# Cross-attention, feed-forward and experts on one core: GpSimd's sequence in a chunk of the first phase

## The reference

```
q, k, v = layernorm(x) @ Wq.T, ctx @ Wk.T, ctx @ Wv.T        # 16 heads of 16, per token
attn    = softmax(q @ k.T / 4)                               # 16 x 16 within one token
x       = x + (attn @ v, heads outermost, reshaped to [128, 256]) @ Wp.T + bp
n       = layernorm(x)
shared  = (silu(n @ sfc1.T) * (n @ sfc2.T)) @ sfc3.T         # 512 hidden
w, e    = top 2 of n @ gate_w.T over 16 experts, softmax over the two
moe     = sum over the two of w * (silu(n @ w1[e].T) @ w2[e].T)   # 128 hidden
out     = x + moe + shared
```

## Time and profile before

| what | value |
|---|---|
| median of three runs | 1799.47 us (1798.7 to 1801.85) |
| the profiled execution | 1810.45 us, span 1808.6 us |
| TensorE busy | 1503.7 us (83%) |
| VectorE busy | 1330.9 us (74%) |
| GpSimd busy | 1348.2 us (75%) |
| ScalarE busy | 725.1 us (40%) |
| DMA | 344.75 MB, mean 191 GB/s |

### The profile page before, as it was taken

The page is one execution under the profiler, slowest core; times in us unless marked ns, Lnnn a source line. Parts: engine busy times, 40 slices in busy tenths (PEclk is TensorE's granted clock), DMA queues, the critical chain, the costliest instruction groups (busy, mean ns, idle before and its releaser), DMA issues.

```text
span 1808.6 us, 50645 instructions
## 1 busy us (share of the span) xinstructions
PE 1503.7 (83%) x17109; PEld 1317.5 (73%) x17110; DVE 1330.9 (74%) x3306; ACT 725.1 (40%) x1346; POOL 1348.2 (75%) x1253
## 2 busy tenths in 40 slices
PE   5499999999999999999999999976677766677674
PEld 4478888778887878778877888765566766677674
DVE  7578888888888888888888888875355555546553
ACT  3244454444544454445444454432232333233231
POOL 4267777777778777777777787866677877778786
PEclk9699999999999999999999999998788898888887
DMA  8788988888889888888888978855777776677673
GB/s 195 142 194 186 183 168 205 198 172 173 181 209 181 180 166 204 194 175 172 180 218 175 180 158 211 168 134 205 238 225 220 228 231 197 188 214 223 210 231 112
DMA packets 945834, 344.75 MB, mean 191 GB/s; under 512 B 824088, under 2 KB 898730, under 8 KB 940288
## 3 DMA queue, kind: packets, MB, share of 16 engines
q1 hardware_dynamic: 901680, 216.53, 58.4%
q0 software_dynamic: 33600, 92.91, 14.5%
q10 hardware_dynamic: 10512, 34.79, 5.9%
HBM read 200.37 MB, written 148.15 MB: 193 GB/s over the span
## 4 chain that ended last, share of the span: by engine, by line
PE 36%; DVE 18%; issue 16%; SPq 9%; POOL 8%; DMA 8%; ACT 4%; DVEq 1%; POOLq 0%; ACTq 0%
PE bank_a L1172 3%; DVE w_sb L786 3%; ACT xn L631 3%; PE bank_y L1159 3%; PE bank_y L1157 3%; PE bank_y L1158 3%; PE bank_a L1157 3%; DVE th L871 2%; DVE ctx_lo L898 2%; PE bank_a L1159 2%; DVE ln_stats L915 2%; PE bank_a L1158 2%; PE bank_u L1157 2%; SPq L337 2%; PE bank_a L1311 2%
## 5 line engine op out<-in xcount | busy, mean ns | idle before, releaser
L400 POOL DMA_INDIRECT slots<-xn,slot_i x256 | 281.3, 1099 | 100.1 <-issue 55.3
L1111 DVE SCALAR_TENSOR_TENSOR v_area<-bank_y,tail,v_area 128x256 f32<-128x256 f32 x288 | 124.4, 479 | 213.5 <-PE bank_y L1159 107.5
L1400 PE MATMUL bank_a<-ident,k_area 128*128 128x128 f32 x576 | 92.8, 313 | 115.9 <-DMA k_area<-slots 115.4
L521 POOL DMA_INDIRECT sums<-v_area,tail x144 | 144.8, 1005 | 57.2 <-issue 35.6
L521 POOL DMA_INDIRECT out<-v_area,tail x144 | 144.8, 1005 | 51.8 <-issue 33.7
L1400 PEld LDWEIGHTS bank_a<-ident,k_area 128*128 128x128 f32 x576 | 74.2, 160 | 126.6 <-DMA k_area<-slots 126.6
L409 POOL DMA_INDIRECT sums<-v_area,slot_i x128 | 128.0, 1000 | 33.1 <-issue 29.2
L1157 PE MATMUL bank_y<-wsh_out_hi,hid_hi 128*128 128x256 f32 x512 | 143.0, 279 | 1.3 <-POOL hid_lo L431 1.3
L1158 PE MATMUL bank_y<-wsh_out_lo,hid_hi 128*128 128x256 f32 x512 | 142.8, 279 | 0.0
L1159 PE MATMUL bank_y<-wsh_out_hi,hid_lo 128*128 128x256 f32 x512 | 142.7, 279 | 0.0
L1157 PE MATMUL bank_y<-w_hi,xn_hi 128*128 x288 | 104.5, 363 | 41.4 <-POOL xn_lo L513 30.0
(11 more groups left out here) (222 smaller groups left out, 5322.8 us busy)
## 6 DMA issues: line engine op xcount, KB each, us to landing
k_area<-slots SPq DMA_DIRECT2D x288, 129.0 KB
v_area<-sums SPq DMA_DIRECT2D x288, 128.0 KB
kv_dram<-w_sb SPq DMA_DIRECT2D x32, 1024.0 KB
x_sb<-in_x_in SPq DMA_DIRECT2D x32, 512.0 KB
ctx_sb<-in_ctx_t SPq DMA_DIRECT2D x32, 512.0 KB
q_dram<-q_sb SPq DMA_DIRECT2D x32, 512.0 KB
k_area<-kv_dram SPq DMA_DIRECT2D x256, 64.0 KB
w_sb<-q_dram SPq DMA_DIRECT2D x256, 64.0 KB
```

Of the source, the lines that this page charges most:

```text
L400: pool.indirect_dma_start(slots[j], bass.IndirectOffsetOnAxis(ap=slot_i[:, par, j, i:i + 1], axis=0), row_of[j][:, i, :], None).then_inc(S ...
L521: pool.indirect_dma_start(target, bass.IndirectOffsetOnAxis(ap=tail[:, r, t, 1 - j:2 - j].bitcast(u32), axis=0), y_ring[:, r, t, :], None, ...
L1111: st = nc.vector.scalar_tensor_tensor(out=y_ring[:, r, t, :], in0=Y[t // 2][:, t % 2 * C:(t % 2 + 1) * C], scalar=tail[:, r, t, j:j + 1], ...
L1400: last = nc.tensor.transpose(A[t // 2][:, t % 2 * C + k * P:t % 2 * C + (k + 1) * P], x_ring[:, r, t, CHANNEL[j] + k * P:CHANNEL[j] + (k + ...
```

## The change

In GpSimd's body the base scatters are cut into one ahead of `xn2_split` and three behind `x_split`; `x_split` moves from the end of body c - 1 (as `x_split(c + 2)` there) to the front of body c (as `x_split(c + 1)`), behind `xn2_split`; all four base scatters stand ahead of `scale_probs`. Of the eight slot scatters three instead of four stand ahead of the first `hid_split`, and one now stands behind the last. On ScalarE `x_round` moves in the same way, from `turned_out` to between the two exponentials of the next body. The prologue no longer has the subtraction and the rounding of chunk 2. No instruction is added or removed, and all data and buffers stay as they were.

```
--- before.py
+++ after.py
@@ -451,35 +451,36 @@
             ln2_power(0)
             ln1_power(2, False)
             ctx_split(2)
-            x_split(2)
-
-            def body(c, par, first, ahead_2):
+
+            def body(c, par, first, ahead, ahead_2):
+                if not first:
+                    scatter_base(c - 2, par, range(1))
                 xn2_split(c - 1)
-                if not first:
-                    scatter_base(c - 2, par, range(3))
+                if ahead:
+                    x_split(c + 1)
+                if not first:
+                    scatter_base(c - 2, par, range(1, BPC))
                 scale_probs(c)
-                if not first:
-                    scatter_base(c - 2, par, range(3, BPC))
-                scatter(c - 1, 1 - par, SCATTERS[:4])
+                scatter(c - 1, 1 - par, SCATTERS[:3])
                 hid_split(c - 1, range(1))
+                scatter(c - 1, 1 - par, SCATTERS[3:4])
+                hid_split(c - 1, range(1, 2))
                 scatter(c - 1, 1 - par, SCATTERS[4:5])
-                hid_split(c - 1, range(1, 2))
-                scatter(c - 1, 1 - par, SCATTERS[5:6])
                 hid_split(c - 1, range(2, 3))
-                scatter(c - 1, 1 - par, SCATTERS[6:])
+                scatter(c - 1, 1 - par, SCATTERS[5:7])
                 hid_split(c - 1, range(3, SB))
+                scatter(c - 1, 1 - par, SCATTERS[7:])
                 ln2_power(c)
                 if ahead_2:
                     ln1_power(c + 2, False)
                     ctx_split(c + 2)
-                    x_split(c + 2)
-
-            body(1, 1, True, True)
+
+            body(1, 1, True, True, True)
             with pool.Fori(2, CHUNKS - 3, 2) as c:
-                body(c, 0, False, True)
-                body(c + 1, 1, False, True)
-            body(CHUNKS - 2, 0, False, False)
-            body(CHUNKS - 1, 1, False, False)
+                body(c, 0, False, True, True)
+                body(c + 1, 1, False, True, True)
+            body(CHUNKS - 2, 0, False, True, False)
+            body(CHUNKS - 1, 1, False, False, False)
 
             def pads(j):
 
@@ -631,12 +632,10 @@
                     st = nc.scalar.activation(xn2[:, i, XN2], h2[:, par, i, :], ACT.Identity, bias=ln2_shift[:, i:i + 1], scale=ln2_rstd[:, i:i + 1])
                 st.then_inc(S["xn2_ready"], 1)
 
-            def turned_out(c, ahead_2):
+            def turned_out(c):
                 for k in range(KT):
                     act.wait_ge(S["t2_full"], at(KT, c, k + 1))
                     nc.scalar.activation(xn2_t[:, k, :], XN2T_BANKS[k][:, :], ACT.Copy).then_inc(S["t2_out"], 1)
-                if ahead_2:
-                    x_round(c + 2)
                 for k in range(KT):
                     act.wait_ge(S["t2_out"], at(KT, c, k + 1))
                     st = nc.scalar.activation(xn2_hi[:, k, :], xn2_t[:, k, :], ACT.Copy)
@@ -664,10 +663,13 @@
             o_round(0)
             ctx_round(2, 0)
             ln2(0, 0, True)
-            turned_out(0, True)
+            turned_out(0)
 
             def body(c, par, first, ahead, ahead_2):
-                exps(c, range(2))
+                exps(c, range(1))
+                if ahead:
+                    x_round(c + 1)
+                exps(c, range(1, 2))
                 gap_exps(c - 1)
                 if ahead:
                     project_out(c + 1, False)
@@ -682,7 +684,7 @@
                     act.wait_ge(S["hid_split"], at(SB, c - 1, 2))
                     load_x_t(c + 2)
                 ln2(c, par, False)
-                turned_out(c, ahead_2)
+                turned_out(c)
 
             body(1, 1, True, True, True)
             with act.Fori(2, CHUNKS - 3, 2) as c:
```

## The result

The changed kernel takes 1959.46 us (median of 4 runs, 1953.35 to 1962.18) against 1799.09 us: a ratio of 1.0886, 95% interval 1.0863 to 1.0908. It is slower by 160 us, where +8.7 was forecast. The profiled execution took 1953.35 us, with a span of 1951.5. One execution of the version with the late gap, further down, took 3583 us, twice its fellows, and is in no ratio here.

The account below looks back on a forecast made before the run. No engine was full, so the order of waits decides, VectorE's queue and `xn` setting the chunk. (0.43 - 0.14) x 30 = +8.7 us gave a median of 1808.2 us; 8 in 10 from 1784 to 1832.

Parts of the forecast that it names:

- Term A: VectorE's small steps from `gap` to L792: holds mostly handed on, -0.14 us a chunk, bounds -0.7 and +0.96.
- term B: `xn` waits for the landing of the slot scatter behind the last `hid` split: +0.43 us a chunk.
- so I take 2.8: Last slot scatter, beside `x_t`'s load: landing taken as 2.8 us after its end, at 633.14 against 632.71 for `xn`.
- the bound of 4.8 us: Last slot scatter's landing: at most 4.8 us after its end, or `xn` would have waited; +2.4 us a chunk there.
- the four: The rival outcomes for the whole kernel: 1787.5, 1795.3, 1841 and 1816 us, chances 0.28, 0.12, 0.12 and 0.08.
- Rival 4: GpSimd's `xn_lo` and `x_lo` not parted by ScalarE's wait (0.8 us), `gap` held: +17, 1816 us; chance 0.08.
- Rival 1: VectorE's holds really go, at `hot` or L861: -0.65 to -0.7 us a chunk there, 1787.5 us; chance 0.28.

Follow-up runs that it names:

- the late gap: The kernel before, with VectorE's `gap` subtraction moved behind the indices and `hot`, a one-column memset in its old place: 1788.84 us, 0.9904.
- the front alone: The changed kernel with all slot scatters where they were before, the new GpSimd front and ScalarE's rounding of x kept: 1814.87 us, 1.0023.
- the late gap and the base scatters together: The kernel before with `gap` behind `hot` and all base scatters ahead of `scale_probs`; three or four slot scatters ahead of the first `hid` split: 0.9807, 0.9811.

## Why the prediction was wrong

**Right.** Term A step by step: `gap` 0.17; `hot` held to 2.25 us; `hot_sum` in its pause at 0.18; the section up to L792 nearly unmoved. I had -0.14 us for the section, and it is +0.05. The rule of the Trainium skill ("SBUF — State Buffer", "SBUF: two separate sides"), two SBUF inputs against a GpSimd subtraction, agrees with the trace here: 2.25 us. The one detail that fell otherwise: the last hold came at `slot_i` (in some chunks at `slot_back`), a few steps ahead of `gap_1`, and ended where it was to end, with `scale_probs`. The mechanism of term B was right as well: `xn` stands behind the eighth scatter's landing.

**Wrong.** The step that failed is the price in term B, "so I take 2.8": the landing came some 5.6 us after the scatter's end (mean over the chunks), and `xn`'s wait grew by 3.44 us, not 0.43. My rows were of a scatter whose packets were out before the x_t load moved. I saw that the new one would lie beside that load, and took a value at the end of the unhindered ones. Even the bound of 4.8 us was none: it bounds the landing of a scatter in front of the load, not of one behind it. The two runs with the transfers held back show it: 4.99 us to the last packet, then 2.86, then 1.76. In the last of them `xn` starts 2.7 us after the scatter's end, so 2.8 was about the price of a scatter with no load in front of it. From the last packet to the start of `xn` it is another 0.8 us in the changed kernel, which my reading of the packets' end as the landing left out too.

**Left out.** That a wait on TensorE costs more than its length. Behind the 3.8 us of idle time ahead of `turn` (80.3 us over 21 chunks) the granted clock is at its lower level, 1.2 GHz, for part or all of the transposes and scores: all of the scores in 10 of the 21 chunks, none in 2, a part in the others. That is 1.80 us a chunk, a third of the loss. In the kernel before TensorE pauses for at most 1.5 us between 200 and 1160 us, and the clock is 1.00 throughout.

**The rivals.** None of the four was it; the forecast's mechanism was, at eight times its price (3.44 us for 0.43), with the clock's 1.80 us on top. Rival 4's worry, the two subtractions side by side in the text, did no harm: they stand apart by ScalarE's wait, 2.6 us in the chunk shown, where I had 0.8: GpSimd waits 2.1 us there on the mean (43.8 us over 21 chunks) behind scores at the lower clock, and 1.0 in the front alone. Rival 1 had the right idea that freed holds pay, but not in this change: it takes the late gap and the base scatters together, -1.9%.

## What to carry to other kernels

A transfer moved behind a large load is priced as queued behind it, not by the landings it had ahead of it; look for what is issued on every other queue in the microsecond before, and for who waits on the landing. Where a buffer is overwritten only when every scatter that reads it has landed, do not put the last of them just ahead of the overwrite. And where a small VectorE step is held by GpSimd, moving GpSimd's work only chooses which step is held; here moving `gap` behind `hot` shortened the hold, and moving `scale_probs` behind the whole run of small steps removed it.

## What the runs showed of the hardware that I had not expected

- A scatter issued 0.2 us behind a 512 KB load has its first packet 3.1 us after its own end on the mean (1.2 for the same scatter in the kernel before), though the DMA engines are not full: in the 2.9 us in which it waits, the load and the v loads take 45% of them.
- A base scatter with `scale_probs` right behind it holds small VectorE steps with two SBUF inputs, but not from its start. In the thirteen traces `hot_sum`, `slot_back` and `slot_i` were requested 155 times up to 0.25 us into such a scatter and took at most 0.18 us; they were requested 293 times at 0.30 to 0.70 us and were held until `scale_probs` ended every time, at least 1.41 us. During a scatter with a pause behind it the same steps ran free wherever they fell (0.16 to 0.23 us).
- TensorE paused inside the scores with no semaphore to wait for and the clock at 1.00: by 1.1 us a chunk in two runs (the eighth scatter put back with the x_t load behind `xn`, and both loads behind `xn`), by 0.26 in the front alone, not at all in the kernel before. The cause is open.
